# An attention and feed-forward kernel: queries of six batches turned through DRAM and VectorE instead of TensorE, with probabilities in PSUM and the widening of weights on ScalarE

## The chip, the core and the metric

The kernel runs on one core of a Trainium2 chip. The metric is device time in microseconds (us), from the start to the end of one execution; the median of three runs counts. The engines are TensorE (in profiles PE, with its weight loads PEld), VectorE (DVE), ScalarE (ACT), GpSimd (POOL) and SyncE (SP). In this kernel SP issues every DMA.

## What is computed

There are 8 batches of 512 rows by 512 columns. Cut to what matters, the reference is:

```
x = x + merge(softmax(where(mask, -1e9, layernorm(x) @ ctx^T / sqrt(512))) @ ctx)   # per batch
    # merge: the attention result transposed, times W_merge^T (512 x 512), plus b_merge
x = x + ffn(layernorm(x))
    # ffn: x quantised with one scale over all batches, gate and up (1408 x 512, int8 rows),
    # silu(gate) * up, quantised again over all batches, down (512 x 1408, int8 rows)
```

## The kernel before

The kernel has two blocks, `attention()` and `ffn()`. T = 4 is the number of 128-row tiles in 512 rows, B = 8 the number of batches n, NI = 11 the number of tiles of the 1408 hidden units. The change lies in the attention block.

All attention products are made from two float32r halves, hi and lo: `product` multiplies hi by hi, hi by lo and lo by hi and adds them in one PSUM bank, so one output tile of 128 x 512 takes 12 matmuls of 128 x 512 (lines 819 to 821) and one 512 x 512 product takes 48. A hi half is a copy that ScalarE makes in float32r, a lo half is the original minus the hi half, made by VectorE or GpSimd.

TensorE's order for batch n (n from 1) is: `scores(n, k)` for k = 0 to 3, `merged(n-1, k)` for k = 0 to 3, then for k = 0 to 3 four transposes of q of the next batch, `transposes(n+1, T+k)` (line 807, into the banks `tr`), and `mixed(n, k)`, the product of the probabilities with W_merge (tiles p and wm). `merged` multiplies the result, g, with the context. All three write the banks `mm[k]`. These waits of TensorE matter:

- `scores(n, k)` waits for `g_ready` of `mixed_lo(n-1, k)` on VectorE, which reads the bank `mm[k]` last, for qT (hi and lo, tile k) and for all of cT (hi and lo).
- `merged(m, 0)` waits for `c_ready` (c_lo of GpSimd), and `merged(n-1, k)` for `masked(n, k)`, which reads the scores out of `mm[k]`.
- `mixed(n, k)` waits for `x1_made(n-1, k)` and, for k = 0, piece by piece for `p_ready`.

Each engine runs its instructions in the order in which they are written, so a waiting instruction holds all behind it. The orders are written out by hand.

- VectorE (lines 676, 598, 604, 573, 585, 608, 615 to 624, 649 to 670, 541, 640): the widening of the last batch's int8 weights to f16 (`weights16(n-1)`), then for each score tile `mask_and_max` (mask added, scaled, row maximum out), the inverse row sum, `probs_lo`, with the row statistics of x of batch n+1 and the turning of its context blocks (`turn_c`, 32 x 32 blocks) between; then four times `add_residual`, `row_stats2`, `row_min2` of batch n-1; `weights_scale(n)`; then alternately `transposed_lo` (qT_lo) and `mixed_lo` (g_lo); last the aggregates.
- ScalarE (lines 434, 441, 424, 463, 473, 417, 448, 430, 483, 487): `exps` and `probs_hi` per tile, then `turned_hi` (cT_hi) and `norm1` (the normalised q, `qn`) of batch n+1 in turn, `context_hi` (c_hi), then for each k `transposed_hi` (qT_hi), `mixed_hi` (g_hi) and `make_mneg` (the mask as bf16), last `weights_round(n)`, which rounds the weights to int8.
- GpSimd (lines 372, 360, 382, 377, 364): `add_bias`, the reciprocal root of the variance (`make_rstd1`, pow), cT_lo in four pieces, c_lo in one instruction of 2048 columns, `make_rstd2` of the batch before.
- SP: the transposing DMAs of the weights (`turn_w`), the loads of mask, weights, x, context rows (`cx`) and context blocks (`cb`), and the stores of the new x (`store_x1`).

The context is transposed in two steps: four DMAs load blocks of it so that each 32 x 32 block only has to be turned where it stands, and VectorE turns the blocks (`turn_c`). The probabilities lie in three SBUF tiles `probs`. An even batch brings two tiles of gate and two of up, an odd batch one of each and one tile of down.

After batch 7 VectorE computes `early_distances`, a part of the first quantisation scale, from the statistics of batches 0 to 6, and then handles the last residuals; the last value leads into the FFN block. In batch 0 all transposes are TensorE's, and `clip_factors` on VectorE follow an exp of ScalarE.

## Time and profile before

| | |
|---|---|
| time, median of 3 runs | 547.75 us (547.31 to 548.17) |
| the profiled execution | 548.55 us, of which span 546.8 us |
| TensorE busy | 529.6 us (97%), 2440 matmuls and transposes |
| VectorE busy | 434.7 us (79%), 805 instructions |
| ScalarE busy | 298.5 us (55%), 445 instructions |
| GpSimd busy | 149.9 us (27%), 100 instructions |
| attention block | 0 to about 301 us |
| FFN block | from about 301 us to the end |

Shares of busy time are averages over the whole span. GpSimd, for instance, works nearly only in the attention block. A matmul's length in the trace is longer than the distance to the next one, because matmuls overlap; the distance from start to start tells what one costs. Idle time of an engine costs something only where another engine waits for it.

### The profile page before, as it was taken

The numbers are of one execution on the slowest core, as the hardware profiler recorded it, in microseconds if no ns is written. First come the engines' busy times: TensorE is split into PE (matmuls) and PEld (weight loads), VectorE is DVE, ScalarE is ACT, GpSimd is POOL, SyncE is SP. The second block draws the span as 40 slices with busy tenths as digits, with TensorE's granted clock in tenths as the row PEclk, the third lists the DMA queues.
The fourth block names the chain that finished last, engine by engine and source line by source line (L and its number), as shares of the span: only waits on it lengthen the run. The fifth ranks groups of instructions, "written<-read, shape, count | busy, mean of one in ns | idle before, by whom it ended". The sixth has DMA issues, their size and how long they took to land. (4 is left out here: it accounts for less than half of the span.)

```text
span 546.8 us, 7319 instructions
## 1 busy us (share of the span) xinstructions
PE 529.6 (97%) x2440; PEld 347.2 (64%) x2440; DVE 434.7 (79%) x805; ACT 298.5 (55%) x445; POOL 149.9 (27%) x100
## 2 busy tenths in 40 slices
PE   5979999999999999999999999999999999999996
PEld 4868888888888888888887444444444444344442
DVE  5586998969889699797668587788778778699984
...
GB/s 277 263 56 154 169 177 173 165 235 169 177 142 181 234 164 178 158 174 77 112 77 180 170 100 296 218 141 326 96 19 38 38 0 59 307 275 397 257 263 154
DMA packets 77599, 93.60 MB, mean 171 GB/s; under 512 B 36096, under 2 KB 54528, under 8 KB 75008
## 3 DMA queue, kind: packets, MB, share of 16 engines
...
q14 instruction: 15, 0.12, 0.1%
...
## 5 line engine op out<-in xcount | busy, mean ns | idle before, releaser
L1257 PE MATMUL gu<-hid,gu_T 128*128 128x512 f16 x704 | 152.3, 379 | 0.5 <-DMA hid<-hid 0.5
L1257 PEld LDWEIGHTS gu<-hid,gu_T 128*128 128x128 f16 x704 | 68.7, 98 | 84.0 <-issue 1.0
L1076 ACT ACTIVATE hid<-gu,gu_mul 128x512 f32<-128x512 f32 x88 | 59.6, 685 | 74.3 <-PE gu L1257 69.8
L1154 DVE SCALAR_TENSOR_TENSOR hid<-gu,gu_mul,hid 128x512 f32 (+1 forms) x88 | 65.0, 746 | 34.0 <-PE gu L1257 30.0
L1298 PE MATMUL gu<-wd_T,gu_T 128*128 128x512 f16 x264 | 58.0, 379 | 1.0 <-DVE gu_T L1198 0.9
L819 PE MATMUL mm<-wm_hi,p_hi 128*128 128x512 f32 x128 | 53.7, 420 | 3.2 <-DVE wm_lo L547 3.2
L1100 ACT ACTIVATE h<-hid,inv 128x512 int8<-128x512 f32 (+3 forms) x32 | 44.2, 1456 | 17.2 <-DVE gu_T L1198 13.4
L1162 DVE TENSOR_REDUCE hmax<-hid 128x1 f32 (+2 forms) x48 | 53.1, 1119 | 0.0
L819 PE MATMUL mm<-cT_hi,qT_hi 128*128 128x512 f32 x128 | 51.1, 399 | 1.9 <-DVE cT_lo L541 1.9
L821 PE MATMUL mm<-wm_hi,p_lo 128*128 128x512 f32 x128 | 51.2, 400 | 0.0
L820 PE MATMUL mm<-wm_lo,p_hi 128*128 128x512 f32 x128 | 50.9, 398 | 0.0
L821 PE MATMUL mm<-cT_hi,qT_lo 128*128 128x512 f32 x128 | 50.4, 393 | 0.0
L820 PE MATMUL mm<-cT_lo,qT_hi 128*128 128x512 f32 x128 | 50.3, 393 | 0.0
L821 PE MATMUL mm<-g_hi,c_lo 128*128 128x512 f32 x128 | 49.8, 389 | 0.0
L819 PE MATMUL mm<-g_hi,c_hi 128*128 128x512 f32 x128 | 49.8, 389 | 0.0
L820 PE MATMUL mm<-g_lo,c_hi 128*128 128x512 f32 x128 | 49.8, 389 | 0.0
L434 ACT ACTIVATE probs<-probs,nmax 128x512 f32<-128x512 f32 x32 | 23.1, 721 | 45.5 <-DVE nmax L598 45.5
L1298 PEld LDWEIGHTS gu<-wd_T,gu_T 128*128 128x128 f16 x264 | 25.5, 98 | 33.0 <-DVE gu_T L1198 2.8
...
L382 POOL TENSOR_TENSOR cT_lo<-cb,cT_hi 128x512 fp32r<-128x512 f32 x28 | 37.9, 1383 | 20.8 <-ACT cT_hi L424 20.7
L377 POOL TENSOR_TENSOR c_lo<-cx,c_hi 128x2048 fp32r<-128x2048 f32 x8 | 37.0, 4621 | 23.6 <-ACT c_hi L473 23.6
L448 ACT ACTIVATE g_hi<-mm 128x512 fp32r<-128x512 f32 x32 | 19.1, 596 | 39.3 <-PE mm L821 39.3
...
## 6 DMA issues: line engine op xcount, KB each, us to landing
...
cb<-in_ctx_dram SPq DMA_DIRECT2D x28, 256.0 KB, 8.4
...
x_dram<-x SPq DMA_DIRECT2D x20, 256.0 KB, 2.4
...
```

What stands on the lines that cost most here:

```text
L377: nc.gpsimd.tensor_tensor(c_lo[:], cx[:], c_hi[:].bitcast(F32), ALU.subtract).then_inc(c_ready, 1)
L382: nc.gpsimd.tensor_tensor(columns(cT_lo, t), blocks(cb[:, t, :]), columns(cT_hi, t).bitcast(F32), ALU.subtract).then_inc(cT_ready, 1)
L434: nc.scalar.activation(probs[t % 3][:], probs[t % 3][:], ACT.Exp, bias=nmax[:, t:t + 1], scale=-1.0, accum_out=rsum[:, t:t + 1]).then_inc( ...
L819: nc.tensor.matmul(bank[:], a_hi[:, t, cols], b_hi[:, t, :], start=t == 0, stop=False)
L820: nc.tensor.matmul(bank[:], a_hi[:, t, cols], b_lo[:, t, :], start=False, stop=False)
L821: last = nc.tensor.matmul(bank[:], a_lo[:, t, cols], b_hi[:, t, :], start=False, stop=t == T - 1)
L1076: nc.scalar.activation(silu[SILU_AT[i]], gu[2 * (i % 3)][:], ACT.Silu, scale=gu_mul[:, 0, i:i + 1]).then_inc(silu_done, 1)
L1100: nc.scalar.activation(h8[:, a:b, :].rearrange("p i l -> p (i l)"), hid[:, slot2(s), a * L:b * L], ACT.Copy, scale=inv[:, 1:2]).then_inc(h ...
L1154: nc.vector.scalar_tensor_tensor(hid[:, b % SLOTS, i * L:(i + 1) * L], gu[2 * (i % 3) + 1][:], gu_mul[:, 1, i:i + 1], silu[SILU_AT[i]], AL ...
L1162: nc.vector.tensor_reduce(hmax[:, k:k + 1], hid[:, b % SLOTS, lo * L:hi * L], AX_X, ALU.max, apply_absolute_value=True).then_inc(hmaxed, 1)
L1257: last = nc.tensor.matmul(gu[2 * (i % 3) + g][:], gu_T[:, g, h, i * P:(i + 1) * P], xT[p][:, h, :], start=h == 0, stop=h == T - 1)
L1298: last = nc.tensor.matmul(yb[T * (s % 2) + t][:], hq[s % 2][:, i, t * P:(t + 1) * P], wd_T[:, i, :], start=i == 0, stop=i == NI - 1)
```

## The change

- q of batches 2 to 7 (`qn`) is stored to a DRAM tensor `q_dram`, row tile by row tile, loaded back in four block DMAs into a new SBUF tile `qb` (`move_q`, on SP), turned there in 32 x 32 blocks by VectorE (`turn_q`), copied to qT_hi by ScalarE (`query_hi`) and subtracted to qT_lo by GpSimd (`query_lo`). The transposes of these batches on TensorE and their `transposed_hi` and `transposed_lo` are gone. q of batches 0 and 1 is turned as before.
- The probabilities of batches 1 to 7 lie in the four PSUM banks `tr`, those of batch 0 in two halves of `qb`.
- GpSimd makes c_lo in four pieces of 512 columns. `make_rstd2` runs once for batches 0 to 6 and once for batch 7.
- The widening of the weights from int8 to f16 moves from VectorE, at the start of the next batch, to ScalarE, right behind the rounding. The int8 and f16 values share the tile `wst`.
- The order on ScalarE, VectorE and SP is another: `norm1` stands ahead of `probs_hi(n, 3)`; two of the four `make_mneg` stand behind the first `exps` of their own batch; `row_bias1` stands further ahead; SP loads the context rows later and x behind the context blocks. The load of `d_scale` stands at the start of the FFN block.

```diff
--- before.py
+++ after.py
+    q_dram = nc.dram_tensor("q_dram", (L, D), F32, kind="Internal").ap()
...
-d_scale = keep("d_scale", [P, D], F32)
+scale_stored = whole.enter_context(nc.semaphore("scale_stored"))
...
+        qb = sb("qb", [P, T, D], F32)
...
-        probs = [sb(f"probs{i}", [P, L], F32) for i in range(3)]
...
-        w8 = sb("w8", [P, WCOLS], I8)
-        wst16 = wst[:].bitcast(F16)
+        wst8, wst16 = wst[:].bitcast(I8), wst[:].bitcast(F16)
...
-        minus_half = sb("minus_half", [P, T], F32)
+        minus_half = sb("minus_half", [P, (B - 1) * T], F32)
...
+        def probs(n, t):
+
+            return tr[t][:] if n else qb[:, t % 2, :]
...
+            def move_q(n):
+                for t in range(T):
+                    sp.wait_ge(q_ready, T * n + t + 1)
+                    if n > 2 and t == 0:
+                        sp.wait_ge(q_moved, 64 * (n - 2))
+                    sp.dma_start(q_dram[t * P:(t + 1) * P, :], qn[:, t, :]).then_inc(q_stored, 16)
+                sp.wait_ge(q_stored, 64 * (n - 1))
+                if n > 2:
+                    sp.wait_ge(qT_ready, T * (n - 2))
+                pieces = q_dram.rearrange("(t k j) (a f) -> a j t k f", j=BLK, k=P // BLK, f=P)
+                for a in range(P // BLK):
+                    sp.dma_start(qb[a * BLK:(a + 1) * BLK, :, :].rearrange("j t (k f) -> j t k f", f=P),
+                                 pieces[a]).then_inc(q_moved, 16)
...
+                    sp.wait_ge(c_ready, T * n)
+                    load_c(n)
                     sp.wait_ge(w_done, through(n - 1, w_turns))
                     load_w(n)
+                    if n < B - 1:
+                        move_q(n + 1)
                     for t in range(T):
                         store_x1(n - 1, t)
                 if n < B - 2:
+                    sp.wait_ge(cT_ready, T * (n + 1))
+                    load_cb(n + 2)
                     if n:
                         sp.wait_ge(min2, T * n)
                         sp.wait_ge(x_free[(n - 1) % 3], 64 * ((n - 1) // 3 + 1))
                     else:
                         sp.wait_ge(wm_done, T)
                     load_x(n + 2)
-                    sp.wait_ge(cT_ready, T * (n + 1))
-                    load_cb(n + 2)
-                if n < B - 1:
-                    sp.wait_ge(c_ready, n + 1)
-                    load_c(n + 1)
...
-            sp.wait_ge(scale_stored, 16 * T)
-            sp.dma_start(d_scale[:], d_scale_dram.rearrange("n r -> (n r)").rearrange(
-                "(a d) -> a d", a=1).to_broadcast([P, D])).then_inc(scale_in, 16)
...
+
+            def make_rstd2(a, b):
+                gp.wait_ge(var2, 1 if a == 0 else 2)
+                nc.gpsimd.tensor_tensor(ln2[:, a:b, 4 * T:5 * T], ve2[:, a:b, :],
+                                        minus_half[:, 0:(b - a) * T].rearrange("p (b t) -> p b t", t=T),
                                         ALU.pow).then_inc(rstd2_made, 1)
...
-                nc.gpsimd.tensor_tensor(c_lo[:], cx[:], c_hi[:].bitcast(F32), ALU.subtract).then_inc(c_ready, 1)
+                for t in range(T):
+                    nc.gpsimd.tensor_tensor(c_lo[:, t, :], cx[:, t, :], c_hi[:, t, :].bitcast(F32),
+                                            ALU.subtract).then_inc(c_ready, 1)
...
+            def query_lo(n):
+                for t in range(T):
+                    gp.wait_ge(qT_hid, T * (n - 2) + t + 1)
+                    nc.gpsimd.tensor_tensor(columns(qT_lo, t), blocks(qb[:, t, :]), columns(qT_hi, t).bitcast(F32),
+                                            ALU.subtract).then_inc(qT_ready, 1)
...
+                    if n:
+                        query_lo(n + 1)
                 make_c_lo(n)
-                if n:
-                    make_rstd2(n - 1)
-            make_rstd2(B - 1)
+            make_rstd2(0, B - 1)
+            make_rstd2(B - 1, B)
...
+            def query_hi(n, t):
+                act.wait_ge(qb_turned, T * (n - 2) + t + 1)
+                if t == 0:
+                    act.wait_ge(s_done, T * n)
+                nc.scalar.activation(columns(qT_hi, t), blocks(qb[:, t, :]), ACT.Copy).then_inc(qT_hid, 1)
...
-                if n and t == 0:
+                if 1 <= n <= 2 and t == 0:
                     act.wait_ge(t_done, T * (n + 1))
+                elif n > 2 and t == 0:
+                    act.wait_ge(q_stored, 64 * (n - 2))
                 q, x_row = qn[:, t, :], xs[n % 3][:, t, :]
-                if n:
+                if n == 1:
                     q = q.rearrange("p (e a i) -> p a e i", e=T, i=BLK)
                     x_row = x_row.rearrange("p (a e i) -> p a e i", e=T, i=BLK)
                 nc.scalar.activation(q, x_row, ACT.Identity, bias=nmr1[:, t:t + 1],
...
-                if n:
-                    act.wait_ge(w16, n)
                 for g in range(2):
                     for i in gu_tiles(n):
                         cols = gu_columns(n, g, i)
-                        nc.scalar.activation(w8[:, cols], wst[:, cols], ACT.Copy,
+                        nc.scalar.activation(as8(cols), wst[:, cols], ACT.Copy,
...
+            def weights16(n):
+
+                act.wait_ge(w_rounded, through(n, rounds))
+                tiles = len(gu_tiles(n))
+                if tiles:
+                    nc.scalar.activation(
+                        wst16[:, 0:4 * tiles * D].rearrange("p (s w) -> p s w", w=2 * D)[:, :, D:2 * D],
+                        wst8[:, 0:8 * tiles * D].rearrange("p (s w) -> p s w", w=4 * D)[:, :, 0:D],
+                        ACT.Copy).then_inc(w16, 1)
+                if n % 2:
+                    cols = down_columns(n)
+                    nc.scalar.activation(as16(cols), as8(cols), ACT.Copy).then_inc(w16, 1)
...
                         probs_hi(n, t)
                         for k in ((0,), (1,), (2, 3), ())[t]:
                             merge_hi(k)
-                    elif t:
-                        probs_hi(n, t - 1)
+                    else:
+                        if t < 2:
+                            make_mneg(n, t + 2)
+                        if t:
+                            probs_hi(n, t - 1)
                 if not start:
+                    if not last:
+                        for t in range(T):
+                            norm1(n + 1, t)
                     probs_hi(n, T - 1)
                 if not last:
-                    for k in range(T):
-                        turned_hi(n + 1, k)
-                        norm1(n + 1, k)
+                    for t in range(T):
+                        turned_hi(n + 1, t)
+                        if start:
+                            norm1(n + 1, t)
                 context_hi(n)
+                if not (start or last):
+                    for t in range(T):
+                        query_hi(n + 1, t)
                 for k in range(T):
+                    mixed_hi(n, k)
                     if start:
-                        mixed_hi(n, k)
                         for g in Q1_AFTER[k]:
                             transposed_hi(n + 1, T + g)
-                    else:
-                        if not last:
-                            transposed_hi(n + 1, T + k)
-                        mixed_hi(n, k)
-                    if not last:
-                        make_mneg(n + 1, k)
+                    if not last and k in (1, 2):
+                        make_mneg(n + 1, k - 1)
                 weights_round(n)
+                weights16(n)
...
+            def turn_q(n, t):
+                if t == 0:
+                    dve.wait_ge(q_moved, 64 * (n - 1))
+                nc.vector.transpose(qb[:, t, :], qb[:, t, :]).then_inc(qb_turned, 1)
...
             def mask_and_max(n, t):
                 dve.wait_ge(s_done, T * n + t + 1)
                 dve.wait_ge(mneg_made, T * n + t + 1)
-                if t >= 3:
-                    dve.wait_ge(p_ready, T * n + t - 2)
+                if n == 0 and t >= 2:
+                    dve.wait_ge(p_ready, t - 1)
+                elif n:
+                    dve.wait_ge(p_ready, T * (n - 1) + t + 1)
                 nc.vector.tensor_tensor_reduce(
-                    out=probs[t % 3][:], in0=mm[t][:], in1=mneg[:, t, :], scale=-SCALE, scalar=-LOWEST,
+                    out=probs(n, t), in0=mm[t][:], in1=mneg[:, t, :], scale=-SCALE, scalar=-LOWEST,
                     op0=ALU.add, op1=ALU.min, accum_out=nmax[:, t:t + 1]).then_inc(masked, 1)
...
-            def variances2(m):
-                dve.wait_ge(row2_made, T * (m + 1))
-                nc.vector.tensor_scalar_add(ve2[:, m, :], means(m)[:, :, 1], EPS).then_inc(var2, 1)
+            def variances2(a, b):
+                dve.wait_ge(row2_made, T * b)
+                nc.vector.tensor_scalar_add(ve2[:, a:b, :], moments(a, b)[:, :, :, 1], EPS).then_inc(var2, 1)
...
-            def weights16(n):
-
-                dve.wait_ge(w_rounded, through(n, rounds))
-                cols = slice(0, w_columns(n))
-                nc.vector.tensor_copy(wst16[:, cols], w8[:, cols]).then_inc(w16, 1)
...
-                dve.wait_ge(rstd2_made, B - 1)
+                dve.wait_ge(rstd2_made, 1)
                 nc.vector.tensor_tensor(high, high, ln2[:, 0:B - 1, 4 * T:5 * T], ALU.mult).then_inc(far_half, 1)
...
-                if not start:
-                    weights16(n - 1)
...
                         if t == 3 and not last:
+                            row_bias1(n + 1)
                             for k in range(T // 2):
                                 turn_c(n + 1, k)
...
                     if not last:
-                        row_bias1(n + 1)
                         for k in range(T // 2, T):
                             turn_c(n + 1, k)
                     probs_lo(n, T - 1)
...
                 weights_scale(n)
+                if not (start or last):
+                    for t in range(T):
+                        turn_q(n + 1, t)
...
                     else:
-                        if not last:
-                            transposed_lo(n + 1, T + k)
                         mixed_lo(n, k)
...
                         aggregate2(n - 1, k)
-                    variances2(n - 1)
-            weights16(B - 1)
+                    if last:
+                        variances2(0, B - 1)
             early_distances()
...
-                    if n > 1:
-                        pe.wait_ge(t_lo, turns(n - 1, g))
-                    elif n == 0 and g == 2 * T - 1:
+                    if n == 0 and g == 2 * T - 1:
...
             def scores(n, k):
                 if n:
                     pe.wait_ge(g_ready, T * (n - 1) + k + 1)
-                pe.wait_ge(t_lo, turns(n, T + k) if n else max(turns(0, T + k), turns(0, T - 1)))
+                if n > 1:
+                    pe.wait_ge(qT_ready, T * (n - 2) + k + 1)
+                else:
+                    pe.wait_ge(t_lo, turns(n, T + k) if n else max(turns(0, T + k), turns(0, T - 1)))
...
                     else:
-                        if not last:
-                            transposes(n + 1, T + k)
                         mixed(n, k)
...
+            sp.dma_start(d_scale[:], d_scale_dram.rearrange("n r -> (n r)").rearrange(
+                "(a d) -> a d", a=1).to_broadcast([P, D])).then_inc(scale_in, 16)
...
+            dve.wait_ge(scale_in, 16)
             nc.vector.tensor_scalar(d_mul[:], d_scale[:], scl[:, 1:2], None, ALU.mult).then_inc(mul_set, 1)
```

## Rows read from the trace of the kernel before

**Rows 1.** Busy time by stretch: us, then PE, PEld, DVE, ACT, POOL, clock, DMA, GB/s.

```profile
46.00:250.70 204.70, 204.70 (x951) 169.36 (x950) 178.62 (x387) 128.86 (x222) 111.38 (x66) 1.00 0.71 176
30.50:36.30 5.80, 5.73 (x14) 4.47 (x15) 4.39 (x14) 1.25 (x2) 1.05 (x1) 0.50 0.00 1
```

**Rows 2.** TensorE in order of time: start us, length us, line, tiles.

```profile
46.38 0.40 PE L820 MATMUL mm<-cT_lo,qT_hi 128*128 128x512 f32 x1
...
115.30 0.39 PE L819 MATMUL mm<-cT_hi,qT_hi 128*128 128x512 f32 x1
...
137.07 0.60 PE L807 MATMUL tr<-ident,qn 128*128 128x128 f32 x4
...
140.28 0.60 PE L807 MATMUL tr<-ident,qn 128*128 128x128 f32 x4
```

**Rows 3.** ScalarE in order of time, batch 0, then the end of batch 2.

```profile
48.59 2.58 ACT L483 ACTIVATE w<-wst,gu_inv 128x512 int8<-128x512 f32 x4
...
115.50 0.60 ACT L448 ACTIVATE g_hi<-mm 128x512 fp32r<-128x512 f32 x1 [1.59 <-PE mm L821]
116.00 0.62 ACT L430 ACTIVATE mneg<-mk 128x512 bf16<-128x512 uint8 x1
116.52 2.55 ACT L483 ACTIVATE w<-wst,gu_inv 128x512 int8<-128x512 f32 x4
```

**Rows 4.** ScalarE groups by form: count, busy us, mean ns of one, idle before.

```profile
L434 ACT ACTIVATE probs<-probs,nmax 128x512 f32<-128x512 f32 x32 | 23.1, 721 | 45.5 <-DVE nmax L598 45.5
...
L441 ACT ACTIVATE p_hi<-probs,rinv 128x512 fp32r<-128x512 f32 x32 | 22.8, 713 | 8.4 <-DVE rinv L604 8.4
...
L463 ACT ACTIVATE qn<-x,nmr,rstd 128x512 f32<-128x512 f32 x20 | 16.1, 803 | 0.1
...
L473 ACT ACTIVATE c_hi<-cx 128x2048 fp32r<-128x2048 f32 x8 | 15.3, 1915 | 8.4 <-PE mm L821 8.4
```

**Rows 5.** VectorE in order of time, batch 3, then the weights of batch 4.

```profile
124.86 0.68 DVE L598 CUSTOM_DVE_ANT_0 probs<-mm,mneg 128x512 f32<-128x512 f32 x1
...
127.33 0.75 DVE L608 SCALAR_TENSOR_TENSOR p_lo<-probs,rinv,p_hi 128x512 fp32r<-128x512 f32 x1
...
128.00 0.68 DVE L598 CUSTOM_DVE_ANT_0 probs<-mm,mneg 128x512 f32<-128x512 f32 x1
...
132.84 0.68 DVE L615 CUSTOM_DVE_ANT_0 x<-mm,x 128x512 f32<-128x512 f32 x1
...
134.76 0.68 DVE L615 CUSTOM_DVE_ANT_0 x<-mm,x 128x512 f32<-128x512 f32 x1
...
175.30 2.27 DVE L649 TENSOR_REDUCE gu_amax<-wst 128x4 f32<-128x2048 f32 x1
...
177.61 0.93 DVE L659 TENSOR_SCALAR gu_scale<-gu_amax 128x4 f32<-128x4 f32 x1
```

**Rows 6.** VectorE, group by form: the turning of the context blocks.

```profile
L585 DVE STREAM_TRANSPOSE cb<-cb 128x512 f32<-128x512 f32 x28 | 18.1, 684 | 0.0
```

**Rows 7.** GpSimd, groups by form: the pow of one and of four columns.

```profile
L364 POOL TENSOR_TENSOR ln<-ve,minus_half 128x4 f32<-128x4 f32 x8 | 8.1, 1010 | 63.5 <-DVE ve L636 63.5
...
L355 POOL TENSOR_TENSOR rstd<-ve,minus_half 128x1 f32<-128x1 f32 x2 | 1.2, 576 | 6.9 <-DVE ve L560 6.9
```

**Rows 8.** VectorE in order of time, the end of the attention part.

```profile
288.04 0.17 DVE L636 TENSOR_SCALAR ve<-ln 128x4 f32<-128x4 f32 x1
...
297.28 0.69 DVE L615 CUSTOM_DVE_ANT_0 x<-mm,x 128x512 f32<-128x512 f32 x1 [0.62 <-PE mm L821]
```

**Rows 9.** GpSimd in order of time, batch 4.

```profile
173.90 4.62 POOL L377 TENSOR_TENSOR c_lo<-cx,c_hi 128x2048 fp32r<-128x2048 f32 x1 [1.27 <-ACT c_hi L473]
```

**Rows 10.** DMA issues: count, KB, median us to landing; from 41 us to 47 us, then over the whole run.

```profile
cb<-in_ctx_dram SPq DMA_DIRECT2D x4, 256.0 KB, 4.7
...
cb<-in_ctx_dram SPq DMA_DIRECT2D x28, 256.0 KB, 8.4
...
x_dram<-x SPq DMA_DIRECT2D x20, 256.0 KB, 2.4
```

36 lines of the change are left out of this document (21 added, 15 removed).

## The prediction

> **What bounds the kernel now.** I read the waits of TensorE first, then its busy time by stretch, then the other engines in order of time over one whole batch. From 46 us to 250.7 us, which is batches 1 to 6 of the attention part, TensorE is busy 204.70 of 204.70 us at the full clock of 2.4 GHz [rows 1]. VectorE (178.62), ScalarE (128.86) and GpSimd (111.38) all have slack there. So in this stretch a product or a transpose taken from TensorE is worth its own time, but only as long as the other engines keep up.
>
> How long is a batch? From the first product of the scores of a batch to the transposes before its merge product there are 96 products in 137.07 - 115.30 = 21.77 us, 0.2268 each [rows 2]. From one group of four transposes to the next there are 12 products more: 140.28 - 137.07 = 3.21 us, of which 12 x 0.2268 = 2.72 are products. A group of transposes thus costs 0.49 us. A batch has 144 products and four groups: 32.66 + 1.92 = 34.58, say 34.56 us.
>
> **What the change takes from TensorE.** The q of batches 2 to 7 is no longer turned there: 6 x 4 groups x 0.48 = 11.5 us. If nothing else waited, a batch would take 32.65 us.
>
> **What it puts in the way.** The order of ScalarE and VectorE decides this. In batch n ScalarE's queue now has, behind the four cT_hi and c_hi, the four pieces query_hi(n+1), and behind them mixed_hi(n, k). VectorE's has weights_scale(n), then the four turn_q(n+1), then mixed_lo(n, k). The scores of batch n+1 start only when g_ready(n, 0) is there, because mixed_lo reads the same PSUM bank. Before, that was long done: the g_hi at 115.50 is the fourth of its batch and TensorE never waited. Now a closed ring forms, because g_hi(n) waits behind query_hi, query_hi waits for VectorE's turn_q, and the exps of the next batch stand behind the weights on ScalarE. I add it up in steps from one start to the next on the same engine, for a batch with four tiles of gate and up:
>
> 1. ScalarE: four g_hi at 0.50 (115.50 to 116.00) and two mneg at 0.52 (116.00 to 116.52) = 3.04; rounding, 2.55 until its end [rows 3] plus 0.04 to notice it = 2.59; the widening to f16, new on this engine: 2048 elements, priced as c_hi with 1.92 less 0.09 overlap [rows 4] = 1.83; exp 0.72; mneg 0.52; exp 0.72; mneg 0.52; p_hi 0.71 + 0.04. Sum 10.69.
> 2. VectorE: p_lo 0.67 (127.33 to 128.00); from mask_and_max to the next with row statistics and the next p_lo between, 3.14 (124.86 to 128.00) [rows 5]; the fourth mask_and_max 0.68 + 0.04. Sum 4.53.
> 3. ScalarE: exp 0.72, p_hi 0.62, four norm1 in a row at 0.80 - 0.09 = 0.71 each (before they stood behind p_hi(3), now ahead of it), p_hi(3) 0.75 [rows 4]. Sum 4.93.
> 4. VectorE: p_lo(3) 0.63; four times residual, statistics and minimum, 4 x 1.92 = 7.68 (132.84 to 134.76); weights_scale 2.31 (175.30 to 177.61) plus 0.30 for its two small steps [rows 5]; four turn_q priced as turn_c, 3 x 0.61 + 0.68 + 0.04 = 2.55 [rows 6]. Sum 13.47.
> 5. ScalarE: the last query_hi 0.52.
>
> The ring is 34.2 us. In the odd batches the rounding and the widening come in unequal pieces and weights_scale has six steps; by the same rows that is about 1.0 us more, so 34.7 us on average. TensorE needs 32.65, so the ring sets the pace and TensorE stands still for about 1.8 us ahead of each batch's scores.
>
> **Probabilities in PSUM.** Five ScalarE instructions of the ring read them. The nearest rows: g_hi from PSUM takes 0.60, mneg of the same size from SBUF 0.62 [rows 3], so 0.02 each for the reading, and perhaps as much for the writing of the exp. Lower bound of the saving 0, upper 0.08 each. I take 0.04, 0.2 us a batch. For VectorE, which writes and reads the bank too, the trace shows no write to PSUM; I put 0, bounds -0.05 to +0.05 for each of five, so +-0.25 a batch. The Trainium skill (VectorE: DVE Perf Modes, section on the TRN2 errata) speaks against this part of the change: it gives VectorE 62 cycles more of fixed cost with a PSUM source than with SBUF, and ScalarE 52 cycles less. By that page the ring would gain 5 x 0.043 and lose up to 5 x 0.065, an estimate of 0.1 us more a batch in place of 0.2 less.
>
> With 0.2 off the ring is 34.5 us against 34.56: batches 2 to 6 give 5 x -0.1 = -0.5 us. The 11.5 us are spent as waiting.
>
> **Batch 1** is worse. Its scores start at 46.38 - 0.23 = 46.15 [rows 2]. In batch 0 the rounding, now behind two mneg instead of four, begins one step of 0.52 earlier than 48.59 [rows 3], at 48.07; widening ends near 52.6, then the exp for the clips, on which VectorE's clip_factors wait, three small steps to 53.2, and mask_and_max(1, 0) stands behind them. The first exp of batch 1 comes at 53.96, 7.8 us after the scores began. In the ring it comes 3.04 + 2.59 + 1.83 = 7.46 after g_hi(n, 0), which itself starts 1.37 (0.60 + 0.69, with 0.04 to notice each) ahead of the scores: 6.1. The rest of the ring is 34.2 - 6.1 = 28.1, with 0.4 for the odd weights_scale and 0.2 off for PSUM 28.3, so batch 1 takes 36.1 us: +1.6.
>
> **The end.** make_rstd2 for batches 0 to 6 is now one instruction over 28 columns. One column takes 0.58, four 1.01 [rows 7], so 0.145 a column more: 4.5 us (bounds: 1.0 if the length cost nothing, 7.1 for seven of four). It starts after the variances, at 288.04 + 0.3 [rows 8], and ends at 292.8; early_distances stand behind it on VectorE with 0.6 us of small steps, and add_residual(7, k) behind those: 293.4, + 1.34, + 2 x 2.09 (1.92 and an aggregate of 0.17) = 298.9, against 297.28 before [rows 8]. +1.6 us, because the distances wait ahead of the residuals. With the lower bound of the price it is 0, with the upper +4.2.
>
> **Edits at nothing.** GpSimd: c_lo in one piece holds it for 4.62 us, and a 4-element tensor_scalar of VectorE issued at 177.61 lasts 0.93, until c_lo's end at 178.52 [rows 5, 9]. The short pieces and the removal of p_lo from that conflict free VectorE, but before, TensorE waited for none of it; in the ring above these steps are already without the conflict. query_lo, at least the 4.6 us of c_lo for as many elements, begins before the scores of the next batch and leaves c_lo some 3 us ahead of merged(n, 0), due 48 products = 10.9 us into that batch. The x loads and the moved d_scale load have tens of us. The weights are loaded from 15 us of the batch on and wanted at 27. If a cover is gone it costs its lateness per batch.
>
> **The sum.** -0.5 + 1.6 + 1.6 = +2.7 us. The profiled execution took 548.55 us (span 546.8), so 551.2 by its own time; it lies 0.8 above the median of the three runs, 547.75. I forecast 547.75 + 2.7 = 550.4 us. Its own range: +-0.25 us for PSUM and +-0.3 for the steps of the ring, over six batches +-3, and the end: 547 to 554.
>
> **Rivals.**
> *A, TensorE still sets the pace (the other sign).* The place is the start of scores(n+1, 0); the price is 547.75 - 11.5 = 536.3 us, and it decides once the ring is under 32.65, 1.8 us less than I add up. Part of it is enough for a gain: each 0.1 us off the ring is 0.6 us, and from 0.65 us off the kernel is faster by over 0.2%. For it speaks that each step was read from a batch in which its engine was not pressed; against it, that every step is a row and none can overlap the next.
> *B, the round trip of q through DRAM is late.* The last norm1 ends 18.1 to 18.7 us into a batch (first exp 6.1 or 6.7, + 3.23 to p_hi(0), + 4.53, + 0.72 + 0.62 + 2.84), its store lands 2.4 after its issue, then four loads go out. With nothing ahead such loads land 4.7 us after their issue, over the whole run the median is 8.4 [rows 10]. So the last, issued some 23.5 us into the batch, has landed between 28.2 and 32 us, and VectorE is ready for it at 29.7 to 30.3. At the late end each batch loses 2 us: 550.4 + 6 x 2 = 562. Before, x and cx share the queue with such loads; here only stores come behind them, so I expect the early end.
> *C, the clock.* After the idle time before 30.5 us TensorE ran at 0.50, its lower level of 1.2 GHz, for 5.8 us [rows 1]. A standstill of 1.8 us a batch could bring that. The scores have about 2 us of cover (mask_and_max(n, 2) waits behind p_lo until 10.0, its product is there at 8.4), so a stretch at half speed of under 4 us costs nothing; 5.8 us would cost 0.9 us a batch, and up to 2 more at the start of the FFN part, where TensorE would stand 1.6 us longer: 556 to 558.
>
> **Chances.** Forecast 0.56; A whole 0.08 and in part 0.13; B 0.11; C 0.12. The measurement cannot tell less than 0.2% (1.1 us) from no change. Faster: A and a little of the forecast, 0.22; same 0.16; slower 0.62. The range to leave out no more than two in ten goes from 543 (the ring 1.2 us shorter) to 557 (part of B or C).
>
> **What would show it.** TensorE's waits should list scores behind VectorE's g_lo, six times, 1.5 to 2 us each (3 for batch 2), and no transposes of qn after batch 1. ScalarE's query_hi should wait some 7 us for VectorE's turn of qb; if that wait is put down to the DMA, B is right. The batches should be 34.3 to 34.7 us apart. The pow of 28 columns should take 4 to 5 us with VectorE idle behind it. The prediction is wrong if TensorE has no waits between batches, or if turn_q starts well before 30 us of the batch.

## The result, and the profile after

The changed kernel takes 564.7 us (median of 6 runs, 560.46 to 565.21) against 547.87 us for the kernel before on the same chip: ratio 1.0298, 95% interval 1.0272 to 1.0324. It is 3% slower. The forecast was 550.4 us with a range of 543 to 557: the direction was right, the size was not. Of all executions below one is in the slower state, one of the six of e6 (566.1 us), and the ratios leave it out.

Busy time by stretch, kernel after, one stretch a batch (us, then PE, PEld, DVE, ACT, POOL, clock, DMA, GB/s; batches 2 to 5), to be read beside the first row of [rows 1]:

```profile
81.48:119.75 38.27, 34.56 (x145) 28.09 (x145) 26.79 (x62) 23.46 (x39) 21.06 (x18) 0.95 0.84 214
119.75:155.74 35.99, 34.40 (x144) 28.02 (x144) 27.29 (x65) 22.90 (x39) 21.03 (x18) 0.96 0.87 234
155.74:192.45 36.71, 32.94 (x144) 26.96 (x144) 26.96 (x62) 23.36 (x39) 21.11 (x18) 0.98 0.88 226
192.45:229.37 36.92, 35.50 (x145) 28.83 (x145) 27.30 (x65) 23.02 (x39) 21.03 (x18) 0.93 0.83 223
```

The transposes are gone (about 144 products a batch are left), but a batch takes 36.0 to 38.3 us in place of 34.56. TensorE stands still, and its clock is no longer full. Its waits, and two of VectorE's, in the view of waits (us in total, times, longest):

```profile
PE mm L881 <- DVE g_lo L711: 18.1, 6, 4.4
...
DVE tr L666 <- PE mm L883: 20.7, 12, 2.8
...
DVE qb L651 <- DMA qb<-q_dram: 9.9, 5, 3.4
```

The first row is the wait that was forecast, six times, but 3.0 us on average where 1.5 to 2 was. The third row stood in rival B: five of VectorE's six turns of q wait for the transfer. The second row looks like rival C, but is not by itself a sign of slow scores: `mask_and_max(n, 0)` and `(n, 1)` wait for their products in every batch, at full clock too. The slow clock, which is C, shows one engine further on, in ScalarE's second exp. Batches 3 (scores at half clock) and 4 (full clock), first TensorE, then VectorE, then ScalarE in order of time:

```profile
119.75 0.80 PE L881 MATMUL mm<-cT_hi,qT_hi 128*128 128x512 f32 x1 [3.71 <-DVE g_lo L711]
120.34 0.63 PE L882 MATMUL mm<-cT_lo,qT_hi 128*128 128x512 f32 x1
120.77 0.63 PE L883 MATMUL mm<-cT_hi,qT_lo 128*128 128x512 f32 x1
...
122.89 0.40 PE L882 MATMUL mm<-cT_lo,qT_hi 128*128 128x512 f32 x1
```

```profile
115.33 2.49 DVE L651 STREAM_TRANSPOSE qb<-qb 128x512 f32<-128x512 f32 x4 [3.36 <-DMA qb<-q_dram]
...
126.99 0.70 DVE L666 CUSTOM_DVE_ANT_0 tr<-mm,mneg 128x512 f32<-128x512 f32 x1 [1.98 <-PE mm L883]
...
151.32 2.49 DVE L651 STREAM_TRANSPOSE qb<-qb 128x512 f32<-128x512 f32 x4 [0.81 <-DMA qb<-q_dram]
...
161.52 0.70 DVE L666 CUSTOM_DVE_ANT_0 tr<-mm,mneg 128x512 f32<-128x512 f32 x1 [1.96 <-PE mm L883]
```

```profile
127.78 0.66 ACT L475 ACTIVATE tr<-tr,nmax 128x512 f32<-128x512 f32 x1 [0.74 <-DVE nmax L666]
...
163.49 0.65 ACT L475 ACTIVATE tr<-tr,nmax 128x512 f32<-128x512 f32 x1
```

In batch 3 `mask_and_max(3, 1)` comes 7.24 us after the first product of the scores, in batch 4 5.78, with the same wait of 2.0 us. The second exp then waits 0.74 us for it in batch 3 and not at all in batch 4.

After the gap the products start every 0.43 us until 122.9, at half clock, then every 0.23 us as before [rows 2]. The q of batch 3 is turned only 33.9 us into batch 2 (115.33 - 81.48). The landing times, DMA issues over the whole run (count, KB, median us), to be read beside [rows 10]:

```profile
q_dram<-qn SPq DMA_DIRECT2D x24, 256.0 KB, 5.2
qb<-q_dram SPq DMA_DIRECT2D x24, 256.0 KB, 5.2
...
x_dram<-x SPq DMA_DIRECT2D x20, 256.0 KB, 6.6
```

The store of q takes 5.2 us, not 2.4. The x1 stores of the same size, which took 2.4, now take 6.6. SyncE's queue in batch 3 shows what lies ahead of q:

```profile
131.70 0.51 SPq L256 DMA_DIRECT2D cx<-in_ctx_dram  x1
132.28 0.48 SPq L289 DMA_DIRECT2D wst<-in_L_ffn_w_gate_dram  x1
132.80 0.43 SPq L289 DMA_DIRECT2D wst<-in_L_ffn_w_up_dram  x1
133.27 0.71 SPq L294 DMA_DIRECT2D wst<-in_L_ffn_w_down_dram  x1
136.35 2.96 SPq L269 DMA_DIRECT2D q_dram<-qn  x4
143.60 1.91 SPq L275 DMA_DIRECT2D qb<-q_dram  x4
```

The last of the four stores is issued by 139.31, the first load 4.3 us later, when it has landed; in batches 2, 4, 5 and 6 it is 7.3, 5.3, 4.4 and 6.8 us. Right ahead of them stand 1 MB of c and 1.2 MB of weights (256, 256 and 704 KB; 1.0 MB in the even batches).

The end came as forecast. GpSimd and VectorE in order of time, answering to [rows 8]:

```profile
302.94 4.81 POOL L389 TENSOR_TENSOR ln<-ve,minus_half 128x28 f32<-128x28 f32 x1 [5.69 <-DVE ve L707]
```

```profile
307.85 0.19 DVE L763 TENSOR_TENSOR far<-far,ln 128x28 f32<-128x28 f32 x1 [4.57 <-POOL ln L389]
...
308.19 0.69 DVE L683 CUSTOM_DVE_ANT_0 x<-mm,x 128x512 f32<-128x512 f32 x1
...
313.52 0.66 DVE L683 CUSTOM_DVE_ANT_0 x<-mm,x 128x512 f32<-128x512 f32 x1
```

From the first product of merged(7, 0) to the first of the FFN part it is 317.31 - 300.84 = 16.5 us; before it was 301.09 - 286.20 = 14.9.

For the comparisons I use one stretch, **M**: from the first product of scores(2, 0) to the first of merged(7, 0) in the profiled execution. That is batches 2 to 6, and the 144 products from scores(7, 0) to the end of mixed(7). M is one execution and not a median: the six of the changed kernel lie between 560.5 and 565.2 us, and M was read in one of 564.96. In e6, whose edit is meant for the end only, M is 217.0. Differences of 2 to 3 us in M are therefore not clear of noise. A **gap** is the distance from the last product ahead to the first of the scores, start to start; it is 0.23 us where TensorE does not stand still. Before: 286.20 - 80.74 = 205.5. The forecast: 5 x 34.5 + 32.65 = 205.2. After: 300.84 - 81.48 = 219.4. So the 14 us that the forecast lacks are lost in M. Batch 1 took 36.98 us (forecast 36.1), but it began 1.65 us earlier (44.50), so that scores(2, 0) came at 81.48 where the forecast says 82.25.

### The profile page after: what moved, and what is told of

It is laid out like the page before. It is cut to its first block and busy times, and to the rows that moved or that the text cites. A ratio compares the mean times of both kernels' runs of the same rounds, so it can differ in the third digit from the quotient of the medians.

```text
span 562.9 us, 7193 instructions
## 1 busy us (share of the span) xinstructions
PE 526.2 (93%) x2344; PEld 341.0 (61%) x2344; DVE 416.4 (74%) x791; ACT 311.9 (55%) x456; POOL 168.3 (30%) x142
## 5 line engine op out<-in xcount | busy, mean ns | idle before, releaser
L881 PE MATMUL mm<-cT_hi,qT_hi 128*128 128x512 f32 x128 | 54.4, 425 | 19.8 <-DVE g_lo L711 18.1
L881 PE MATMUL mm<-wm_hi,p_hi 128*128 128x512 f32 x128 | 50.8, 397 | 4.0 <-DVE wm_lo L608 3.5
L1167 ACT ACTIVATE h<-hid,inv 128x512 int8<-128x512 f32 (+3 forms) x32 | 44.2, 1455 | 17.2 <-DVE gu_T L1266 13.4
L883 PE MATMUL mm<-cT_hi,qT_lo 128*128 128x512 f32 x128 | 52.6, 411 | 0.0
L882 PE MATMUL mm<-cT_lo,qT_hi 128*128 128x512 f32 x128 | 52.4, 410 | 0.0
L410 POOL TENSOR_TENSOR cT_lo<-cb,cT_hi 128x512 fp32r<-128x512 f32 x28 | 35.5, 1302 | 33.9 <-ACT cT_hi L459 33.8
L416 POOL TENSOR_TENSOR qT_lo<-qb,qT_hi 128x512 fp32r<-128x512 f32 x24 | 30.0, 1280 | 52.3 <-ACT qT_hi L471 52.3
L404 POOL TENSOR_TENSOR c_lo<-cx,c_hi 128x512 fp32r<-128x512 f32 x32 | 40.3, 1295 | 14.7 <-ACT c_hi L516 14.7
L881 PEld LDWEIGHTS mm<-cT_hi,qT_hi 128*128 128x128 f32 x128 | 25.9, 202 | 27.8 <-DVE g_lo L711 20.6
```

The lines of the kernel that those rows point to most:

```text
L404: nc.gpsimd.tensor_tensor(c_lo[:, t, :], cx[:, t, :], c_hi[:, t, :].bitcast(F32), ALU.subtract).then_inc(c_ready, 1)
L410: nc.gpsimd.tensor_tensor(columns(cT_lo, t), blocks(cb[:, t, :]), columns(cT_hi, t).bitcast(F32), ALU.subtract).then_inc(cT_ready, 1)
L416: nc.gpsimd.tensor_tensor(columns(qT_lo, t), blocks(qb[:, t, :]), columns(qT_hi, t).bitcast(F32), ALU.subtract).then_inc(qT_ready, 1)
L881: nc.tensor.matmul(bank[:], a_hi[:, t, cols], b_hi[:, t, :], start=t == 0, stop=False)
L882: nc.tensor.matmul(bank[:], a_hi[:, t, cols], b_lo[:, t, :], start=False, stop=False)
L883: last = nc.tensor.matmul(bank[:], a_lo[:, t, cols], b_hi[:, t, :], start=False, stop=t == T - 1)
```

## The experiments

Three theories. **1**: q lands late. **2**: the order of ScalarE and VectorE, the ring, is longer than I added up. **3**: the half clock after a standstill makes the scores slow and so the ring longer. Each run has beside it runs of the kernel before on its own chip; the ratio is to those. The edits are to the changed kernel, where no other run is named.

### First round: one cause at a time

**e1_q_from_input**
```diff
-  pieces = q_dram.rearrange("(t k j) (a f) -> a j t k f", ...)    # behind the four stores
+  pieces = context[n].rearrange("(t k j) (a f) -> a j t k f", ...) # ahead of them
```


> The changed kernel, but the buffer that VectorE turns is filled from the context input (same blocks, same bytes) ahead of the stores of q, so nothing waits for the round trip; the stores of q to DRAM stay. Left out: the scores of batches 2 to 7 are made from the context in place of q. Theory 1 (the round trip lands late and holds turn_q for 2 us a batch): turn_q no longer waits for the DMA, the batches come down from 37 to 34.5 to 35 us, the kernel to 551 to 555 us. Theory 2 (the order of ScalarE and VectorE is the bound, the DMA lands inside slack that the ring has anyway): 560 or more. Theory 3 (the low clock after the standstills lengthens the scores and the ring): the wait for g_lo shrinks by the 2 us of the DMA but about half the loss stays, 556 to 560.


Measured: 557.4 us, 1.0203 (1.0168 to 1.0238), M 211.7. No turn of q waits any more, and M is 7.7 us shorter, so about half of the loss hangs on q. The time fell in the range of theory 3 and not in that of theory 1. From batch 2 on the lengths are 34.82, 36.58, 34.82, 34.60, 36.43, and in the two long batches VectorE now waits for x, 6.3 us in all (1.3 more in batch 5), which none of the theories had.

**e2_q_store_queue**
```diff
-  sp.dma_start(q_dram[...], qn[:, t, :])
+  nc.scalar.dma_start(q_dram[...], qn[:, t, :])     # behind each norm1
```


> The changed kernel, with the four stores of q of a batch issued by ScalarE behind each norm1, on its own DMA queue, in place of SyncE's queue, where the loads of c and of the weights stand ahead of them. If the stores are late because they stand behind those loads in one queue: they land in 2.5 to 3.5 us in place of 5.2, the loads of qb go out 1.5 to 2.5 us earlier, and the kernel takes 555 to 560 us. If the queues share the DMA engines so that the order makes no difference: 564 as before. If the issue costs ScalarE time in the ring (four issues a batch between the norm1): up to +0.5 us a batch, 565 to 568.


Measured: 566.9 us, 1.0352 (1.0314 to 1.0390), M 219.3. The stores land in 4.2 us in place of 5.2, but ScalarE pays for it, as its order of time shows:
```profile
135.37 0.80 ACT L501 ACTIVATE qn<-x,nmr,rstd 128x512 f32<-128x512 f32 x1
136.21 0.33 ACTq L507 DMA_DIRECT2D q_dram<-qn  x1
136.58 0.82 ACT L501 ACTIVATE qn<-x,nmr,rstd 128x512 f32<-128x512 f32 x1 [0.41 <-ACT qn L501]
```
From one norm1 to the next it is now 1.21 us in place of 0.71. 4 x 0.5 = 2 us more in the ring eat the 1 us of the store and more: q's turn waits only 0.5 us in all, yet batches 2 to 6 take 36.4 to 37.8 us. These 2 us are four times the price that I had put on it.

**e3_g_before_q**
```diff
   for k in range(T): mixed_hi(n, k)
+      if k == 1: for t in range(T): query_hi(n + 1, t)   # likewise turn_q behind mixed_lo(n, 1)
```


> The changed kernel, with query_hi behind mixed_hi(n, 1) on ScalarE and turn_q behind mixed_lo(n, 1) on VectorE, so that g_lo(n, 0) no longer waits for four turns and four query_hi. Theory 2 (the order is the bound): TensorE's wait goes from g_lo to qT_lo and becomes shorter, 33.5 to 35 us a batch, 546 to 556 us. Theory 1 (the landing of q is the bound): scores(n+1) then wait for qT_lo, which comes some 2.5 us after the landing (0.62 turn, 0.60 query_hi, 1.28 query_lo): the batches come down by 1 to 2.5 us all the same, since five of the eight small steps leave the way between landing and scores, 550 to 558. Neither (the feedback runs through slow scores, theory 3): over 560.


Measured: 560.4 us, 1.0231 (1.0167 to 1.0295), M 214.7. The scores now start as GpSimd has made the first low piece of q, and the wait became shorter (gaps 1.1 to 4.1 us). Theories 1 and 2 had both foretold 558 or less, so it tells them not apart, and falls just into the third case.

**e5_fill_clock**
```diff
+  for _ in range({1: 12, 2: 14, 3: 6, 4: 14, 5: 6, 6: 16}.get(n, 0)):
+      nc.tensor.matmul(tr[3][:], wm_hi[:, 0, 0:P], wm_hi[:, 0, :], start=True, stop=True)
```


> The changed kernel, with 6 to 16 products into an unused PSUM bank behind mixed(n, 3), as many as fill most of the wait ahead of scores(n+1, 0); nothing reads them. Theory 3 (the low clock after the standstills feeds the ring): the granted clock stays at 1.00 through all batches, mask_and_max no longer waits for TensorE, each of six batches is 1 to 1.5 us shorter, 555 to 559 us. Theories 1 and 2 (the clock only eats cover): the clock stays up and the time at 563 to 566.


Measured: 561.1 us, 1.0259 (1.0229 to 1.0289), M 214.3. In the profiled execution the span's clock is 0.997 in place of 0.979, and M is 5.1 us shorter, although the 14 and 16 products were too many: behind batches 2, 4 and 6 they fill the whole gap and nothing else is waited for. But that execution (558.4 us) is the fastest of five. By the ratios the gain is 0.4%, some 2 us, and the intervals of this run and the changed kernel overlap. The median lies between the 555 to 559 of theory 3 and the 563 to 566 of the others, so this run by itself does not show what the clock costs.

### Second round: two causes together, and the order again

**e8_input_and_fill** (both edits; 10 products behind batch 1, 6 behind the others)


> The two edits of the runs before together: the turned buffer filled from the context input (left out: the scores of batches 2 to 7 are made from the context in place of q) and 6 products (10 behind batch 1) into an unused PSUM bank behind mixed(n, 3). If the late round trip and the low clock are all that the prediction's sum lacked: granted clock 1.00 in every batch, no wait for g_lo beyond 2 us after batch 1, batches 34.5 to 34.8 us apart, and the kernel at the forecast of 550 to 552 us. If a third term of the ring is missing: batches over 35 us at full clock, 553 or more.


Measured: 556.9 us, 1.0162 (1.0145 to 1.0179), M 210.1. Two batches are there (34.36, 34.14), three are not (37.05, 35.77, 36.01), with the span's clock at 0.994. The one of 35.77 follows a gap of 2.23 us behind which the clock fell in spite of the products (0.62). In the other two something third was missing, and the trace names it, VectorE in order of time:
```profile
128.01 1.29 DVE L632 BATCH_NORM_STATS2 st<-x 128x6 f32<-128x512 f32 x2 [3.74 <-DMA x<-in_x_dram]
```
The x of the next batch is late. SyncE waits in this run, as in the changed kernel, for q's stores to land before it stores x1, and the load of x stands behind that.

**e4_widen_vector**
```diff
-  weights16(n)            # ScalarE, behind weights_round(n)
+  weights16(n - 1)        # VectorE, behind mask_and_max(n, 0)
```


> The changed kernel, with the widening of the weights to f16 on VectorE again, behind mask_and_max(n, 0), in place of ScalarE ahead of the exps. If the widening of 1.9 us ahead of the first exp is in the ring, as the prediction had it: the first exp of a batch comes 1.8 us earlier and the kernel is 1 us a batch shorter, 557 to 561 us. If slow scores or the landing of q hide it: 563 to 566. If VectorE's widening delays mask_and_max(n, 1) by more than that: 567 or more.


Measured: 571.1 us, 1.0424 (1.0403 to 1.0444), M 221.3. The widening takes 1.92 us there too in a batch with four tiles, and about 3 us in two pieces in the others. I had a gain as the first case and this loss as the third, and the trace bears the third out: in all six batches ScalarE's second exp waits 1.2 to 2.5 us for `mask_and_max(n, 1)`, which stands behind the widening. The turns of q wait for the DMA 11.9 us in all in place of 9.9.

**e9_g_first_fill_rstd2** (the edit of e3; 4 to 8 products; variances and pow per batch, as in e6 below)


> The changed kernel with three edits: query_hi behind mixed_hi(n, 1) and turn_q behind mixed_lo(n, 1); 4 to 8 products into an unused bank behind mixed(n, 3); variances and pow of the second normalization made per batch as before. If the gains stand beside each other (5 us for the order, 5 us for the clock, 1.6 us for the end): 552 to 555 us. If order and clock pay for the same stall: 555 to 558. The end alone shows in the time from merged(7, 0) to the FFN part: 14.9 us in place of 16.5.


Measured: 557.9 us, 1.0186 (1.0165 to 1.0206), M 213.6; the end is 14.9 us. The clock is at 1.00 behind every gap, and M is still 213.6, against 214.7 and 214.3 for order and products alone: the two do not add up, they pay for the same stall.

**e10_c_load_earlier** (on e9)
```diff
+  if g and n < B - 1: load_c(n + 1)      # between the transposes of gate and of up
```


> The run before, with the load of c of the next batch issued between the weight transposes of gate and up in place of behind them and behind the mask, about 3 us earlier, so that 1 MB is out of the way of the stores of q. If the stores are late because of the loads ahead of them: they land 1 to 1.5 us earlier and five batches are each 0.7 to 1.5 us shorter, 3 to 7 us less than that run. If the weight loads alone (1.3 MB, still right ahead) make them late: the same time within 1 us.


Measured: 572.7 us, 1.0457 (1.0435 to 1.0479), M 227.3, 15 us slower than e9. Both theories were wrong. SyncE's queue shows why:
```profile
90.41 1.39 SPq L256 DMA_DIRECT2D cx<-in_ctx_dram  x1
91.85 1.20 SPq L303 DMA_TRANSPOSE gu_T<-wst  x1
93.08 8.17 SPq L307 DMA_TRANSPOSE wd_T<-wst  x1
```
The last transposing transfer behind the load holds the queue for 8.17 us (5.21 and 9.04 in the other two batches that have it) where the same transfer took 1.45. The one right behind the same load took 1.20, as ever, so it is not shown what exactly holds it. All that stands behind it, the weights and q, comes later.

### Third round: SyncE's order, and the end

**e11_input_fill_free_queue** (on e8)
```diff
-  sp.wait_ge(q_stored, 64 * (n - 1))      # in move_q; now once, at the end of the queue
```


> The run with the input and the fill, and SyncE no longer waits for the stores of q to land before it goes on to the stores of x1, the load of the context blocks and the load of x (the wait stands at the end of the queue only). Left out as there: the scores of batches 2 to 7 are made from the context in place of q. In that run VectorE waited up to 3.7 us for x in two batches. If this (x behind the round trip in SyncE's order) is the third term: no wait of the row statistics for x beyond 0.5 us, batches 2 to 6 at 34.4 to 34.8 us, the kernel at 549 to 553 us. If the x load is late for another reason (its own release by the stores of x1): the wait stays and the time is 555 to 557.


Measured: 550.2 us, 1.0058 (1.0036 to 1.0079), M 204.4. No wait for x is left, and batches 2 to 6 take 34.25 to 34.36 us. The load of x behind the round trip was the third term of those runs. (In the changed kernel itself VectorE does not wait for x from batch 1 on.)

**e12_p_first**
```diff
+  probs_hi(n, T - 1)
   for t in range(T): norm1(n + 1, t)
-  probs_hi(n, T - 1)
```


> The changed kernel with p_hi(n, 3) ahead of the four norm1 of the next batch on ScalarE. VectorE then has p_lo(3), and all that is behind it, 1.36 us earlier (its idle time there), while q is 0.57 us later. If the ring of ScalarE and VectorE sets the pace: 1.0 to 1.4 us a batch less, 556 to 559 us. If the landing of q sets it in most batches: 0 to 0.6 us a batch more, 564 to 568.


Measured: 562.9 us, 1.0302 (1.0248 to 1.0356), M 215.1. It lies between the two cases, its runs are wide apart (559.8 to 567.9), and its ratio is that of the changed kernel. The wait for q's transfer grows from 9.9 to 15.3 us: most of what VectorE wins it waits. The stores of q, issued later behind the same loads, land in 3.2 us (median) in place of 5.2, so q wins back there a part of what it is made later.

**e13_p_first_all** (that order on e9, with 8 products behind batch 1 and 4 behind the others)


> The same order (p_hi(n, 3) ahead of the norm1) on top of the three edits together (query behind the second mixed tile, products that fill the wait, now 4 and 8 behind batch 1, rstd2 per batch), which gave 557.9. There q lands some 2 us before VectorE turns it, so the 1.36 us should be kept nearly whole: 34.4 to 35 us a batch, 549 to 553 us. If the landing of q is the next to bind at once: 555 to 558.


Measured: 556.4 us, 1.0153 (1.0120 to 1.0186), M 214.7. Two batches at 35.1 and 34.8 us, then one of 37.9, in which VectorE waits 2.05 us for x and 3.07 for q. The stores of q land in 2.8 us. The landings bind at once.

**e6_rstd2_per_batch**
```diff
-  gp: make_rstd2(0, B - 1)      # once, behind the loop      dve: if last: variances2(0, B - 1)
+  gp: if n: make_rstd2(n - 1, n)                             dve: variances2(n - 1, n)
```


> The changed kernel with the variances and the pow of the second normalization per batch as before. If the price at the end is as forecast: the pow of 28 columns (4.8 us) goes, merged(7, 0) to the FFN part takes 14.9 us in place of 16.5, and the kernel 1.6 us less, 562 to 564. If the pow per batch (1.0 us of GpSimd, and a small VectorE instruction that may stand still under GpSimd's hold) costs the ring 0.2 to 0.3 us a batch: no change, 564 to 566.


Measured: 562.2 us, 1.0251 (1.0211 to 1.0292). From merged(7, 0) to the FFN part it is 314.31 - 299.41 = 14.9 us. All seven runs with this edit have 14.9, and all the others but e4 (16.8) have 16.5: the 1.6 us of the end are shown there, though the ratios of e6 and the changed kernel overlap.

### Fourth round: the ring by itself, and what makes q late

**e14_ring_alone** (e11 without the products in the gap)


> The run with the input and the free queue, without the products that filled the wait. Left out as there: the scores of batches 2 to 7 are made from the context in place of q. There each batch from 2 on was 34.26 to 34.36 us, which is just 32.65 and six products, so the true ring may be shorter. If the ring is 34.3 us as forecast: gaps of 1.6 us, no fall of the clock from batch 2 on, the same 549 to 551 us. If the ring is shorter than that: gaps of 0.3 to 1.2 us, and 543 to 548, at the speed of the kernel before or faster.


Measured: 551.3 us, 1.0071 (1.0045 to 1.0097), M 206.0. Batches 3 to 6 take 34.24, 34.36, 34.24, 34.36 us, with gaps of 1.70 and 1.82 us at full clock. That is the ring of the prediction, with nothing in its way. Batch 2, which starts at half clock, took 35.98 us, 1.6 more than in e11, and ScalarE's second exp waits 1.50 us in it: that is the price of this fall of the clock. The granted clock stands in the windows behind the gaps (3.56, 0.66, 1.70 us):
```profile
81.70:84.70 3.00, 3.00 (x7) 2.42 (x8) 2.22 (x7) 3.00 (x7) 3.00 (x3) 0.50 1.08 268
117.68:120.70 3.02, 3.02 (x13) 2.52 (x14) 2.21 (x7) 3.02 (x7) 3.02 (x3) 1.00 1.17 209
151.92:154.90 2.98, 2.98 (x13) 2.49 (x14) 2.21 (x7) 2.98 (x7) 2.98 (x3) 1.00 1.14 198
```

**e15_quarter_context**
```diff
-  sp.dma_start(cx[:], ctx_t[n])                          # 1 MB
+  sp.dma_start(cx[:, 0:1, :], ctx_t[n][:, 0:1, :])       # 0.25 MB; likewise the blocks in cb
```


> The changed kernel, in which from batch 1 on (context blocks: from batch 2 on) the loads of c and of the context blocks bring a quarter of their bytes, in the same number of transfers, in the same places of the queue: 1.5 MB a batch less. Left out: three quarters of the later batches' context, old values stand in. If q is late because the DMA engines are loaded (0.88 of the batch): its stores land in 3 to 4 us in place of 5.2, its loads in 4 to 4.5, and the kernel takes 556 to 560 us. If the order of the queue or the landing time of a lone transfer makes it late: 563 to 565.


Measured: 556.1 us, 1.0154 (1.0118 to 1.0190), M 209.8. Here q makes its whole round trip, and batches 3 to 5 still come down to the ring: 34.67, 34.37, 34.24. (Batch 6 takes 36.13 with a wait of 1.7 us for q, and batches 2 and 7 start at half clock.) The turns wait for the DMA 2.0 us in all in place of 9.9. DMA issues:
```profile
q_dram<-qn SPq DMA_DIRECT2D x24, 256.0 KB, 3.2
qb<-q_dram SPq DMA_DIRECT2D x24, 256.0 KB, 4.7
```
The order and the number of transfers are the same, so the bytes of the others make q late. Which of the two loads, c or the context blocks, counts more is not shown.

**e16_q_within_sbuf** (on e13, with 6 and 3 products) and **e17_q_within_sbuf_alone** (on the changed kernel)
```diff
+  for k in range(4):
+      for a in range(4):
+          sp.dma_start(qb[a*BLK:(a+1)*BLK, :, k*P:(k+1)*P], qn[k*BLK:(k+1)*BLK, :, a*P:(a+1)*P])
```


> The run with p_hi(n, 3) ahead of the norm1 and the three edits, in which q goes from qn to qb in 16 transfers of 64 KB inside the on-chip memory (q_dram is not used), 3 products behind mixed(n, 3) (6 behind batch 1). One landing in place of two and 1 MB less. Issuing 16 transfers takes SyncE some 7.7 us (0.48 each), so q has landed some 10.5 us behind the last norm1 in place of 13.3. If the landing sets the pace there: 34 to 35 us a batch, 546 to 552. If SyncE's 7.7 us push the stores of x1 and the load of x back and these bind: 553 or more.

> The changed kernel with only that: q from qn to qb in 16 transfers inside the on-chip memory. If the round trip through DRAM is the largest loss: VectorE's turn no longer waits for the DMA (9.9 us over the run before), 557 to 561 us. If the many issues cost as much: 563 to 566.


Measured: e16 562.4 us, 1.0294 (1.0249 to 1.0339), M 219.5; e17 558.0 us, 1.0207 (1.0171 to 1.0244), M 209.3. Alone it helps, the turns wait 2.9 us in all. On e13, where q is made later, it hurts: the 16 issues take SyncE 11.1 us (0.69 each, I had 0.48), and q (13.0 us of waits) and x (10.7) both come later. SyncE's queue in e16:
```profile
141.01 11.09 SPq L270 DMA_DIRECT2D qb<-qn  x16
```

### Fifth round: can the whole kernel come down to the ring?

**e18_q_sbuf_fill_rstd2** (e17, 4 and 8 products, rstd2 per batch)


> The changed kernel with q moved inside the on-chip memory (which alone gave 558.0), 4 products behind mixed(n, 3) (8 behind batch 1) and rstd2 per batch. If each cause is worth what it showed alone: the clock 2 to 4 us, the end 1.6 us, so 552 to 555 us with batches near the ring's 34.3 us. If the many issues on SyncE make the load of x late once the batches are shorter: 556 to 558.


Measured: 554.9 us, 1.0141 (1.0116 to 1.0167), M 211.1. The time is at the upper end of what was added up. M is not shorter than in e17 (209.3, read in the fastest of its four executions), so the traces do not show the clock's share.

**e19_halves_x1_on_scalar** (on e13, with 6 and 3 products)
```diff
+  for h in range(2):                       # rows 0 and 1, then 2 and 3
+      sp.wait_ge(stored[h], 32 * (n - 1))
+      for a in range(4): sp.dma_start(qb[..., some, :], pieces[a][:, some]).then_inc(moved[h], 16)
-  sp: store_x1(n - 1, t)
+  act: the same four stores behind mixed_hi(n, 1)
```


> The run with p_hi(n, 3) ahead of the norm1 and the three edits (556.4), with the loads of qb in two halves (rows 0 and 1 as soon as their stores have landed), and the stores of x1 of batches 0 to 6 issued by ScalarE in its idle time behind mixed_hi(n, 1), so that SyncE comes to the load of x earlier. If the landings bind there: the first half of q lands 3 to 4 us earlier, 34 us a batch or less, 543 to 550 us, and it may beat the kernel before. If the load on the DMA engines binds, whatever the order: both halves land as late as before, 554 to 558.


Measured: 548.7 us, 1.0036 (1.0007 to 1.0064), M 204.1. Batches 2 to 6 take 34.22 to 34.32 us, the DMA waits are gone (0.8 us for q, 0.4 for x), at the full load of transfers. DMA issues:
```profile
q_dram<-qn SPq DMA_DIRECT2D x24, 256.0 KB, 3.3
qb<-q_dram SPq DMA_DIRECT2D x48, 128.0 KB, 3.1
...
x_dram<-x ACTq DMA_DIRECT2D x16, 256.0 KB, 5.7
```
So the load on the DMA engines is no wall: the order and the cutting of the transfers decide with it. The stores' 3.3 us are not this edit's doing (e13 had 2.8); new are the halves and the free queue for x, and the run does not tell the two apart. Nor is its 34.3 us the ring of the prediction again, since the order of ScalarE and VectorE is another: here the scores start 0.1 us behind GpSimd's first low piece of q. It wins back 16 of the 17 us, and does not beat the kernel before. No kernel tried here does.

## Why the prediction missed

**Right.** TensorE's saving is real and can't be used: the forecast ring of 34.5 us was measured as 34.24 and 34.36 (e14), and the whole kernel without the late transfers at 551.3 and 550.2 us against the 550.4 forecast. The wait ahead of the scores was put on g_lo, where it is. The end was forecast at +1.6 us and measured at 16.5 - 14.9 = 1.6 (e6 takes it away), the pow at 4.5 and measured at 4.81. In batch 1 the first exp was forecast for 53.96 us and came at 53.24, and the scores of batch 2 follow 28.24 us behind it (forecast 28.3). That the scores of batch 1 began 1.65 us earlier was not forecast, and is worth nothing, since the exp sets the place. Two small slips in the ring's sum change it by 0.1 us or less: the listed steps add up to 34.14, not 34.2, and six of its steps on ScalarE read PSUM, not five.

**Probabilities in PSUM.** The exp takes 0.66 us (0.72 before), p_hi 0.68 (0.71), so 0.035 to 0.06 each where 0.04 was taken. VectorE writes them in 0.70 (0.68) and reads them in 0.75, as before [rows 5]: of the fixed cost of 62 cycles that the Trainium skill gives for a PSUM source (VectorE: DVE Perf Modes, section on the TRN2 errata) p_lo shows nothing. The step was right and small.

**The step that failed** is in rival B: "its store lands 2.4 after its issue", and "here only stores come behind them, so I expect the early end". The norm1 end where forecast (135.51 + 2.92 - 119.75 = 18.7 us into batch 3, by ScalarE's order of time), but the stores land in 5.2 us, the first load goes out 4.3 to 7.3 us behind the issue of the last store, and q can be turned at 31.6 to 33.9 us (115.33 - 81.48, 151.32 - 119.75) where VectorE is ready at 30.0 to 31.9. I looked at what comes behind the transfers, not at what lies ahead of them: 1 MB of c, which this change itself moves there, and 1.0 to 1.2 MB of weights. e15 shows the bytes as the cause, e19 that another order with smaller pieces takes the wait away at the same bytes. The sign that I had named for B could not show it either: ScalarE's query_hi waits 49.1 us in six times, all put down to VectorE's turn, and it is the turn that waits for the DMA.

**The second failure** is that B and C were weighed as separate cases, and C from a standstill of 1.8 us. The ring by itself (e14) has gaps of 1.70 and 1.82 us, 1.5 to 1.6 of them standstill, behind batches 3 to 6, and the clock stays up. Only behind batch 1, with its 3.6 us, does it fall, and not in every run (e12 and e17 start batch 2 at full clock behind 3.8 and 3.6 us). With the DMA's waits on top the gap ahead of the scores is 4.1 to 4.8 us three more times, and each time the scores start at half clock. Then "the scores have about 2 us of cover" fails too. It was worked out for mask_and_max(n, 2), but it is mask_and_max(n, 1) that comes first: at full clock it starts 5.8 us after the scores, and the second exp, 0.8 us behind it, would start at 7.2 to 7.8 us anyway. That is 0.6 to 1.2 us of cover, and behind the falls of the clock the mask came 1.3 to 2.6 us later.

**The sum.** The five batches of M can be taken apart: the measured ring of 34.3 us, the wait of the turn for q, and the rest.

| batch | gap ahead | clock, first 3 us | first two exps wait | turn waits for q | length | less 34.3 and the wait for q |
|---|---|---|---|---|---|---|
| 2 | 3.58 | 0.57 | 0.35 | 3.36 | 38.27 | 0.6 |
| 3 | 4.10 | 0.50 | 0.74 | 0.81 | 35.99 | 0.9 |
| 4 | 1.98 | 1.00 | 0 | 2.24 | 36.71 | 0.2 |
| 5 | 4.16 | 0.50 | 1.74 | 0.62 | 36.92 | 2.0 |
| 6 | 1.80 | 1.00 | 0 | 2.90 | 37.36 | 0.2 |

Where the clock stayed up, ring and wait give the length to 0.2 us; where it fell, 0.6 to 2.0 us are left, and all but 0.2 to 0.3 of that is the wait of ScalarE's exps for the late scores. The stretch of batch 7 adds 34.1 - 32.65 = 1.5 behind its gap of 4.81. Together: 9.9 us of waits for q and 3.9 + 1.5 = 5.4 for the rest, mostly the clock, less 5 x 0.2 for a ring shorter than forecast: 14.3, of 14.2 measured. The experiments agree as far as they go: one fall costs 1.6 us (e14 against e11), while holding the clock gave back 5.1 in the profiled execution of e5 but only some 2 by its median. The share of the clock thus rests on the traces, not on a difference of times. Taking the round trip away gave 7.7 (e1), and 13.4 once x and SyncE's order were free too (e14), since with q in time three of the four falls don't happen either.

**Edits at nothing.** "The x loads have tens of us" held in the changed kernel as it is. As soon as the batches came near 34 us, x was late by up to 3.7 us (e8), since SyncE reaches its load behind q's round trip.
